# A ternary-weight feed-forward kernel: h0 of all groups before the first y tile, ternary weights by ScalarE and VectorE alone, y tiles two ahead, and the output read once from PSUM

## What is computed

```python
q_emb = relu(cond @ W3 + b3)                        # one row of 512 per batch
x1 = (n * x + sum(x, axis=1)) * q_emb[:, None, :]   # n = 64
h0 = relu(x1 @ W2 + b2)                             # 2048 rows of 512

def ternary(w):                                     # groups of 64 weights, read as bf16
    scale = clip(mean(abs(w)), 1e-8)
    return clip(round(w / scale), -1, 1) * scale

h  = square(relu(h0 @ ternary(W_fc).T))             # 2048 x 2048
hn = h * rsqrt(mean(square(h), axis=-1) + eps)
out = x + hn @ ternary(W_proj).T                    # 2048 x 512
```

## Time and profile before

| what | us |
|---|---|
| device time, 3 runs | 360.41 to 360.49, median 360.49 |
| span of the profiled execution | 357.6 |
| device time over the span (median less span) | 2.9 |
| PE busy | 326.9 (91% of the span) |
| DVE busy | 222.9 (62%) |
| ACT busy | 181.7 (51%) |
| POOL busy | 164.4 (46%) |

### The profile page before, as it was taken

The page is one execution under the profiler, slowest core; times in us unless marked ns, Lnnn a source line. Parts: engine busy times, 40 slices in busy tenths (PEclk is TensorE's granted clock), DMA queues, the critical chain, the costliest instruction groups (busy, mean ns, idle before and its releaser), DMA issues.

```text
span 357.6 us, 4131 instructions
## 1 busy us (share of the span) xinstructions
PE 326.9 (91%) x1350; PEld 242.7 (68%) x1350; DVE 222.9 (62%) x285; ACT 181.7 (51%) x272; POOL 164.4 (46%) x103
## 2 busy tenths in 40 slices
PE   6995869967869599999999999999999999999995
PEld 6544657554446478878867678788666688888884
DVE  0799999999999933487732123777722224465325
ACT  1775767767575355445443335545434354544550
POOL 2376656776657822333434442333434333344350
PEclk9996998989989899999999999999999999999999
DMA  7971055334411520000070000001120000000403
GB/s 221 378 286 59 0 120 148 88 88 101 100 36 29 159 105 2 0 31 31 29 256 10 0 0 0 0 29 59 49 98 0 0 0 2 29 31 31 147 0 117
DMA packets 24991, 25.66 MB, mean 72 GB/s; under 512 B 13424, under 2 KB 14480, under 8 KB 24976
## 3 DMA queue, kind: packets, MB, share of 16 engines
q1 hardware_dynamic: 23920, 25.47, 22.7%
q10 hardware_dynamic: 1056, 0.00, 0.2%
HBM read 18.39 MB, written 4.19 MB: 63 GB/s over the span
## 4 chain that ended last, share of the span: by engine, by line
PE 62%; DVE 28%; issue 7%; POOL 1%; ACT 1%; DVEq 0%; POOLq 0%; ACTq 0%
PE ps_out L360 26%; PE ps_acc L342 25%; DVE w_tern L481 8%; PE ps_x L321 8%; DVE y_hi L515 6%; DVE abs_sum L465 5%; DVE h_hi L504 2%; PE ps_out L302 1%; DVE x_t L496 1%; DVE y_lo L517 1%; DVE scale L468 1%; DVE w_mask L471 1%; PE ps_x L373 1%; POOL w_signed L722 1%; DVE rsq L529 1%
## 5 line engine op out<-in xcount | busy, mean ns | idle before, releaser
L232 POOL TENSOR_TENSOR sq_acc<-sq_acc,y_sq 128x512 f32<-128x512 f32 x55 | 89.2, 1623 | 108.9 <-ACT y_sq L650 108.7
L360 PE MATMUL ps_out<-w_t,y_hi 128*128 128x512 f32 x256 | 109.6, 428 | 19.2 <-DVE y_lo L517 18.0
L515 DVE CAST y_hi<-y 128x512 fp32r<-128x512 f32 x64 | 42.3, 661 | 100.3 <-ACT y L643 100.2
L360 PE MATMUL ps_out<-w_t,y_lo 128*128 128x512 f32 x256 | 103.9, 406 | 0.0
L342 PE MATMUL ps_acc<-h_hi,w_t 128*128 128x512 f32 (+1 forms) x256 | 103.7, 405 | 0.0
L342 PE MATMUL ps_acc<-h_lo,w_t 128*128 128x512 f32 (+1 forms) x256 | 102.7, 401 | 0.0
L636 ACT ACTIVATE relu_y<-ps_acc 128x512 f32<-128x512 f32 x64 | 38.2, 597 | 116.6 <-PE ps_acc L342 116.3
L360 PEld LDWEIGHTS ps_out<-w_t,y_hi 128*128 128x128 f32 x256 | 49.2, 192 | 36.5 <-DVE y_lo L517 22.3
L722 POOL TENSOR_TENSOR w_signed<-w_sign,scale 128x1024 bf16<-128x1024 bf16 x16 | 46.1, 2881 | 42.8 <-DVE scale L468 40.0
L342 PEld LDWEIGHTS ps_acc<-h_hi,w_t 128*128 128x128 f32 x256 | 50.0, 195 | 12.8 <-issue 0.6
L360 PEld LDWEIGHTS ps_out<-w_t,y_lo 128*128 128x128 f32 x256 | 49.5, 194 | 12.9 <-issue 1.9
(11 more groups left out here) (59 smaller groups left out, 210.4 us busy)
## 6 DMA issues: line engine op xcount, KB each, us to landing
raw<-in_L_ffn_W_fc_dram SPq DMA_DIRECT2D x8, 512.0 KB, 3.7
raw<-in_L_ffn_W_proj_dram SPq DMA_DIRECT2D x8, 512.0 KB, 4.9
x_res<-in_x_dram SPq DMA_DIRECT2D x4, 1024.0 KB, 5.8
out_dram<-o_sb SPq DMA_DIRECT2D x16, 256.0 KB, 2.0
x_sb<-in_x_dram SPq DMA_DIRECT2D x3, 1024.0 KB, 8.1
x_sb<-in_x_dram SPq DMA_DIRECT2D x4, 256.0 KB, 4.5
wv_sb<-in_L_cond_W_dram SPq DMA_DIRECT2D x2, 512.0 KB, 7.9
o_sb<-in_L_cond_W_dram SPq DMA_DIRECT2D x1, 512.0 KB, 5.5
```

The source lines that it names most:

```text
L232: engine.tensor_tensor(sq_acc[:], sq_acc[:], y_sq[:, j % SQ_RING, :], ALU.add).then_inc(sq_added, 1)
L360: last = pe.matmul(ps_out[:, t, :], part[:, j % RING, t * P:(t + 1) * P], w, start=(j == 0 and part is y_hi), stop=(j == HJ - 1 and part i ...
L515: dve.tensor_copy(y_hi[:, j % RING, :], y[:, j % RING, :]).then_inc(hi_done, 1)
```

## The change

- h0 of all four groups (16 units, u = 0..15) is made first, then the 64 tiles (v = 0..63) run without h0 work between them. `h0_hi` and `h0_lo` hold four groups; `x1_t` has two buffers; `ps_acc` has three banks; loops are written out.
- In the list of each of ACT and DVE a **step** i stands at units 0, 1, 2, 4, 5, 8, 9, 12, 13, 14, 15 (steps 0 to 10) and at tiles 0, 2, 4, 6, 8 (steps 11 to 15). DVE's step i sums pair i+1 and makes pair i ternary; ACT's step i spreads the scale of pair i+1 over 64 columns each (`spread_pair`, new), reads pair i+2 and keeps pair i-1. `w_scale` takes the place of `w_signed`, and POOL has no part in the weights. The compare is a plain `tensor_tensor` with the spread scale, and a second and third one multiply by sign and scale. The PE transposes are gone: all 16 pairs are turned by DMA.
- `raw` has 2 buffers instead of 4. `load_pair(i + 2)` and `turn_pair(i)` alternate in SP's list, with the loads of x for groups 2 and 3 and the residual of group 0 between them.
- `hidden` runs two tiles ahead of `project`.
- `finish` reads `ps_out` directly, all four t in a row, behind `split_y` of the group's second tile; `project` of the next group's first tile waits for it. `copy_even` and `copy_odd` are gone.
- Several SBUF tensors share room (`o_sb`, `relu_y`, `y` in `x1_t`, `y_sq` and `sq_acc` in `wv_sb`, `x_res` in `x_sb`).

```diff
-SQ_RING = 4
-RAW_RING = 4
+RAW_RING = 2
+READ_RING = 3
+ACC_RING = 3
+SQ_RING = 2
+AHEAD = 2
...
-        PAIRS += [fc_pair(2 * c), proj_pair(c, 0), proj_pair(c, 1), fc_pair(2 * c + 1)]
-    EARLY = 4
-    ON_PE = set(range(EARLY)) | {len(PAIRS) - 1}
+        PAIRS += [fc_pair(2 * c), fc_pair(2 * c + 1), proj_pair(c, 0), proj_pair(c, 1)]
+    SUMS_AT = 2
+    STEP_AT_UNIT = {0: 0, 1: 1, 2: 2, 4: 3, 5: 4, 8: 5, 9: 6, 12: 7, 13: 8, 14: 9, 15: 10}
+    STEP_AT_TILE = {0: 11, 2: 12, 4: 13, 6: 14, 8: 15}
...
@@ block.sync
+            load_pair(1)
+            load_x(1)
+            for i in range(len(PAIRS)):
+                if i + RAW_RING < len(PAIRS):
+                    load_pair(i + RAW_RING)
+                turn_pair(i)
+                if i == 2:
+                    load_x(2)
+                if i == 4:
+                    load_x(3)
+                if i == 7:
+                    load_res(0)
...
@@ block.tensor
+            def project_tile(v, t):
...
+                if j == 0:
+                    wait(pe, finished, TT * (g - 1) + t + 1)
...
+            for u in range(UNITS):
+                if u % KD == SUMS_AT and u // KD + 1 < GROUPS:
+                    sum_x(u // KD + 1)
+                make_h0(u)
+            for v in range(AHEAD):
+                hidden(v)
+            for v in range(TILES):
+                if v + AHEAD < TILES:
+                    hidden(v + AHEAD)
+                if v % HJ == HJ - 1:
+                    sum_squares(v // HJ)
+                project(v)
...
@@ block.vector
+            def sum_pair(i):
+                dve.wait_ge(abs_ready, i + 1)
+                wait(dve, scale_ready, i)
+                dve.tensor_reduce(abs_sum[:], grouped(w_abs[:, i % READ_RING, :]), AX.X, ALU.add).then_inc(sum_ready, 1)
+                dve.wait_ge(sum_ready, i + 1)
+                wait(dve, spread_ready, i - RING + 1)
+                dve.tensor_scalar(scale[:, i % RING, :], abs_sum[:], 0.5 / TERN_GROUP, MIN_SCALE,
+                                  ALU.mult, ALU.max).then_inc(scale_ready, 1)
+            def ternary_pair(i):
+                dve.wait_ge(spread_ready, i + 1)
+                wait(dve, tern_ready, i)
+                dve.tensor_tensor(w_mask[:], w_abs[:, i % READ_RING, :], w_scale[:, i % RING, :], ALU.is_gt).then_inc(masked, 1)
+                dve.wait_ge(masked, i + 1)
+                dve.wait_ge(sign_ready, i + 1)
+                dve.tensor_tensor(w_mask[:], w_mask[:], w_sign[:, i % READ_RING, :], ALU.mult).then_inc(picked, 1)
+                dve.wait_ge(picked, i + 1)
+                wait(dve, turned, 16 * (i - RING + 1))
+                dve.tensor_tensor(w_tern[:, i % RING, :], w_mask[:], w_scale[:, i % RING, :], ALU.mult).then_inc(tern_ready, 1)
+            def step(i):
+                if i + 1 < len(PAIRS):
+                    sum_pair(i + 1)
+                ternary_pair(i)
...
+            for u in range(UNITS):
+                g, m = u // KD, u % KD
+                if u > 0:
+                    round_h0(u - 1)
+                if g + 1 < GROUPS and m >= SUMS_AT:
+                    for k in range(2 * (m - SUMS_AT), 2 * (m - SUMS_AT) + 2):
+                        scale_x(g + 1, k)
+                if u in STEP_AT_UNIT:
+                    step(STEP_AT_UNIT[u])
+            round_h0(UNITS - 1)
+            for v in range(TILES):
+                split_y(v)
+                if v in STEP_AT_TILE:
+                    step(STEP_AT_TILE[v])
+                if v % HJ == AHEAD - 1 and v >= HJ:
+                    inverse_root(v // HJ - 1)
+                    finish(v // HJ - 1)
...
@@ block.scalar
+            def spread_pair(i):
+                act.wait_ge(scale_ready, i + 1)
+                wait(act, tern_ready, i - RING + 1)
+                act.activation(w_scale[:, i % RING, :].rearrange("p (s w) -> p s w", w=TERN_GROUP),
+                               scale[:, i % RING, :].rearrange("p (s o) -> p s o", o=1).to_broadcast([P, SG, TERN_GROUP]),
+                               ACT.Copy).then_inc(spread_ready, 1)
+            def step(i):
+                if i + 1 < len(PAIRS):
+                    spread_pair(i + 1)
+                if i + 2 < len(PAIRS):
+                    read_pair(i + 2)
+                if i > 0:
+                    keep_pair(i - 1)
+            for u in range(UNITS):
+                if u > 0:
+                    relu_h0(u - 1)
+                if u in STEP_AT_UNIT:
+                    step(STEP_AT_UNIT[u])
+            relu_h0(UNITS - 1)
+            for v in range(TILES):
+                hidden_tile(v)
+                if v in STEP_AT_TILE:
+                    step(STEP_AT_TILE[v])
```

More of the change, by code:

```diff
@@ new lines, in project_tile, with project @@
+                for part in (y_hi, y_lo):
+                    last = pe.matmul(ps_out[:, t, :], part[:, v % RING, t * P:(t + 1) * P], w,
+                                     start=(j == 0 and part is y_hi), stop=(j == HJ - 1 and part is y_lo))
+                if j == HJ - 1:
+                    last.then_inc(tile_summed, 1)
+                return last
+            def project(v):
+                g, j = v // HJ, v % HJ
+                if g == 0 and j % TT == 0:
+                    pe.wait_ge(wt_ready, ready_pairs(HJ + KD * (j // TT) + 2))
+                pe.wait_ge(split, v + 1)
+                for t in range(TT):
+                    last = project_tile(v, t)
@@ L430, in _ @@
                 for k in range(KD):
[L431 removed]
+                    last = sum_x_block(t, k)
                     if t == TT - 1:
                         last.then_inc(xt_done, 1)
[L435 to L441 removed]
@@ L442, in _ @@
-            hidden(0, 0)
-            group(0, range(EARLY - 1, len(PAIRS)), True)
-            with pe.Fori(1, GROUPS - 1) as g:
-                group(g, [], True)
-            group(GROUPS - 1, [], False)
+            for u in range(UNITS):
[10 more added lines that the diff above has]
+                project(v)
@@ L582, in _ @@
+                wait(dve, stored, 16 * TT * g)
+                for t in range(TT):
+                    dve.wait_ge(tile_summed, TT * g + t + 1)
+                    dve.scalar_tensor_tensor(out=o_sb[:, t, :], in0=ps_out[:, t, :], scalar=rstd[:, t:t + 1],
+                                             in1=x_res[:, t, :], op0=ALU.mult, op1=ALU.add).then_inc(finished, 1)
             dve.wait_ge(condt_done, 1)
@@ L613, in read_pair @@
             def read_pair(i):
[L615 removed]
                 act.wait_ge(raw_loaded[i % RAW_RING], 16 * (i // RAW_RING + 1))
[L617 to L620 removed]
+                wait(act, masked, i - READ_RING + 1)
@@ new lines, in read_pair @@
+                act.activation(w_abs[:, i % READ_RING, :], raw[:, i % RAW_RING, :], ACT.Abs, scale=2.0).then_inc(abs_ready, 1)
+                wait(act, picked, i - READ_RING + 1)
+                act.activation(w_sign[:, i % READ_RING, :], raw[:, i % RAW_RING, :], ACT.Sign).then_inc(sign_ready, 1)
+            def spread_pair(i):
[4 more added lines that the diff above has]
+                               ACT.Copy).then_inc(spread_ready, 1)
```

486 lines of the change are left out of this document (146 added, 340 removed).

## The result

| | before | changed |
|---|---|---|
| device time, median | 360.49 us (360.41 to 361.58, 5 runs) | 392.82 us (390.15 to 393.99, 5 runs) |
| span of the profiled execution | 357.6 | 388.4 |
| device time of the profiled execution | not listed | 390.15 |
| PE busy | 326.9 | 335.5 |
| DVE busy | 222.9 | 215.4 |

The ratio is 1.088 (95% interval 1.084 to 1.091): slower, by 32 us, where 27.5 were forecast. All times here are of fast executions; a slow one of run 8, of 814.6 us, is left out, and what slowed it is not known. The page of the changed kernel: busy time of each engine, then PE's and ACT's busy tenths and PE's granted clock in 40 slices of 9.7 us.

What follows compares the result with a forecast made beforehand. DVE was taken to bound the old kernel's first stage, PE its second. Terms 126.6 + 39.0 + 202.7 + 3.2 + 8.7 + 4.9 gave a 385.1 us span, plus 2.9 for the median: 388.0, range 369 to 402.

Steps and rivals of the forecast that it cites:

- The h0 stage: From the start through all 16 h0 units: project of tile 0 forecast at 126.6 us, PE mostly waiting.
- The keeps: ACT's keeps of w_t in the h0 stage: first ends at 27.1 us, nine intervals of 95.8, last at 122.9.
- The two prices that rested on an estimate or a remote row: ACT's spread of the scale taken as 1.04 us; keep to keep with a 1 MB load in between, 11.4.
- this ring: h0 stage: load waits behind transpose, transpose for an earlier keep, keep for its load; 8.0 or 8.6 us keep to keep.
- the clock: Slow PE clock, costing nothing as forecast; throughout tiles 0 to 8, 5.4 us more (393.4), within a rival of chance 0.18.
- Tiles 0 to 8: First tiles, still with weight steps, ACT late: 39.0 us instead of 29.8.
- Group ends: Next group's tile 0 waits for the finish of each bank: loss 2.9 us, three times, 8.7.
- The tail: End of the kernel, after the last full project: 4.9 us from its end.
- Span to median: 2.9 us between span and median of the runs, added to the 385.1 span to give 388.0.
- The signs: Keeps at 27 to 123, PE half busy to 126, seven raw waits, three 3 us finish waits; wrong if other waits follow tile 8.
- loads don't wait: Rival for the h0 stage: loads land as ACT wants them, 18.5 us less, 369.5; chance 0.13.
- The rival on the other side: Lists run ahead and PE bounds the h0 stage: project 0 at 83.9 us, total 336; chance 0.04.

Runs made afterwards that it cites:

- run 8: Changed kernel with loads a step earlier, finish a tile earlier, ACT reading and keeping before spreading, plus loads of group 2's x and group 0's residual moved later: 345.67 us.
- run 1: Changed kernel with each pair's load sent one step earlier in SP's list, ahead of the transpose: 372.72 us, ratio 1.035.
- run 6: Changed kernel with three extra unused fp32 matmuls on PE ahead of each h0 unit from the fourth on: 392.75 us, ratio 1.087.
- run 7: Changed kernel without POOL's additions of squares, except the first of each group and the very last: 388.77 us, ratio 1.077.
- run 10: Changed kernel with ten extra unused small matmuls on PE ahead of the first project of groups 1 to 3: 389.96 us, ratio 1.082.
- run 2: Changed kernel with 1/rms and finish behind the split of the next group's first tile instead of its second: 383.52 us, ratio 1.064.
- Run 4: Changed kernel with three edits together (loads a step earlier, finish a tile earlier, ACT reading and keeping before spreading): 344.05 us, ratio 0.954.
- run 3: Changed kernel with ACT's step reordered to read, keep, spread instead of spread, read, keep: 388.97 us, ratio 1.079.

## Why the prediction was right

The time (388.0, range 369 to 402) was 4.8 us under the median and the direction right; step by step:

- **The h0 stage**, forecast 126.6: 126.55. The keeps were forecast at 27, 35, 46, 55, 71, 79, 95, 106, 115, 123, and end at 27.8, 36.1, 47.5, 55.8, 71.1, 79.2, 94.4, 105.8, 114.4, 122.3. All are within 1.5 us of the list. The two prices that rested on an estimate or a remote row hold: 11.37 for the step with a megabyte in between, the spread at 1.05. Runs 1 and 6 show that it is this ring and not the clock. That the sum agrees to 0.1 is luck: the first keep came 0.7 late and the way from the last keep to tile 0 took 0.5 more, and the nine intervals took 1.3 less, all of it where `scale_x` stands in between (15.2 for 15.9, twice).
- **Tiles 0 to 8**, forecast 39.0: 40.2, and 0.8 more at the next two. `y_lo` beside POOL's addition takes about 1.7; I had allowed for POOL once, at unit 15, and not in each of these tiles. Run 7 prices it at 3.6 over ten tiles, or about 2.9 over the eight.
- **Group ends**, forecast 8.7: 9.0, of which 3 x 2.57 = 7.7 are the wait itself (1.83 for the first bank, the rest between the banks). The finish takes 0.68 a bank, also where POOL adds beside it. The remaining 1.3 are one fall of the clock, behind the second of the three pauses.
- **The tail**, forecast 4.9: 5.5 from the end of the last project. From the first project matmul behind the squares to the end of the span it is 7.6 where the trace of before gave 6.85; the finishes start 0.2 later, and from their start to the end it takes 5.9 instead of 5.25.
- **Span to median.** The span was forecast at 385.1 and is 388.4: 1.2 + 0.8 in the tiles, 0.3 at the ends, 0.6 in the tail, the rest in the tiles behind. The 2.9 added for the median didn't hold: the median lies 4.4 above the span, 1.75 between span and device time of one execution, and 2.7 by which the median lies over the profiled execution, the fastest of the five. In the other sets, where span and device time of each execution of the kernel before are listed, they lie 1.8 to 2.0 apart, so the 2.9 was itself some 1.9 and a remainder that belongs to the execution profiled. Of the 2.7, run 10 puts a part down to the clock at group ends; a later end of the h0 stage (0.9 to 1.4 in the traces of runs 2, 6, 7 and 10) can be the other, and the executions without a trace don't say how they divide.
- **The terms that were mis-sized** are thus two, both small. The sum counted DVE's wait for POOL at unit 15 and at the group ends and not in tiles 0 to 10, which took 2.0 more. And the prediction named the clock only for the first stage and for tiles 0 to 8, where it costs nothing, and gave it nothing behind the pauses that the change itself creates, where a fall costs 1.3.
- **The signs.** The keeps came as listed. PE was busy 72% of the h0 stage and not about half of it. ACT's waits for `raw` were ten, of 0.2 to 4.9 us and 18.1 in all, six of them of about 1.5 and more, where seven of 2 to 5 were named. The three waits for the finish were 1.8 and not 3. And PE waited once more behind tile 8, 0.5 us for `y_lo` of tile 9, which the prediction had called a sign of being wrong: run 7, without the additions, has no such wait there.

Of the rivals, "loads don't wait" (18.5 less, 369.5) was priced well: made real in run 1 it wins 20.1 and gives 372.7. The rival on the other side, PE as the bound of the h0 stage (336), needs ACT to clip h0 without waiting for a step, and no run made that real. Run 4 comes to 344, with the finish out of the way, but its tile 0 is projected at 97.0 and not at 83.9, and PE is busy 71.8 us of the 84 from 13 to 97: lists and loads still hold it.

## What to carry to other kernels

When several in-order lists pass work round, write down the ring, that is, the way from an instruction back to itself one step later. Price an edit against the ring, not against the wait that it removes: run 3 took away 36.6 us of waiting and won 3.9, and the same edit won 19.9 with the other ring open. Ask of each load whether it stands behind something that itself waits for the use of an earlier load; here the order of two entries in a queue was worth 20 us, at no cost in buffers. And a pause of 2 us in PE in an otherwise full stage can cost more than 2 us, because the clock may fall behind it: fill it, or better, remove it.

## What the runs showed of the hardware

- **DVE beside POOL.** A timeline of DVE at a group end; POOL adds from 188.26 to 189.77 and from 195.72 to 197.01:

```profile
188.66 1.67 DVE L440 TENSOR_TENSOR y_lo<-x_t,y_hi 128x512 fp32r<-128x512 f32 x1
191.90 0.43 DVE L438 CAST y_hi<-x_t 128x512 fp32r<-128x512 f32 x1 [1.58 <-PE ps_out L322]
192.36 0.69 DVE L440 TENSOR_TENSOR y_lo<-x_t,y_hi 128x512 fp32r<-128x512 f32 x1
196.49 0.81 DVE L438 CAST y_hi<-x_t 128x512 fp32r<-128x512 f32 x1 [3.43 <-PE ps_out L322]
197.33 0.69 DVE L440 TENSOR_TENSOR y_lo<-x_t,y_hi 128x512 fp32r<-128x512 f32 x1
```

  The subtraction that starts inside the addition ends 0.56 after it (it takes 0.69 alone), and so does the cast (0.29 after; 0.43 alone). All 45 subtractions of the trace that start inside an addition take 1.66 to 1.75 and end 0.54 to 0.56 behind it. It isn't a slower rate, it is a wait for the other's end. The Trainium skill (SBUF — State Buffer, "SBUF: two separate sides") describes an exclusive lock of a shared port pair, taken for a whole instruction by who starts first; the trace agrees. The finish reads one operand from PSUM and one from SBUF, and at 199.17 its four take 2.73 together although POOL adds from 200.27 on. In the last group, with POOL idle, they take 2.72.
- **The clock behind a short pause.** PE idled 1.83 us, with 8 matmuls of one column 6 us before; afterwards the granted clock stayed in two of three cases, and fell to its lower level (1.2 GHz) for some 3 us in the third (0.91 over the 18 us shown for run 10). Over five traces it fell at 8 of 15 such pauses. Ten small matmuls in the gap kept it up at all three. The Trainium skill (TensorE: Matmul & The Clock Gate, "Part 1: The HAM clock gate") says of the rise of the clock at a kernel's start that the same kernel reaches it after a different number of matmuls from run to run. It doesn't say so of pauses; here the fall behind a pause differs in the same way from one group end to the next.
- **1 MB ahead of 512 KB.** Sent 0.6 us behind a load of 1 MB, a load of 512 KB lands 6.4 us after its issue (38.11 in the chain above); alone 4.0 (48.86).
